# A cross-attention and ternary feed-forward kernel on one core: new hand-written orders for all engines, new PSUM banks, and a finer warm-up

## The chip, the cores and the metric

The kernel runs on one core of a Trainium2 chip. The metric is the device time of one execution in microseconds; the time of a kernel is the median of its runs. One execution of each kernel is also recorded by the hardware profiler, and the views below come from that execution. Engines are called by their names in the profile: PE is TensorE's matmuls, PEld its weight loads, DVE is VectorE, ACT is ScalarE, POOL is GpSimd, SP is SyncE, which only issues transfers.

## The reference, cut to what matters

Eight batches of 256 rows and 512 columns. A linear attention against a context, then a feed-forward block with ternary weights:

```
q, k, v = heads(norm(x) @ Wq + bq), heads(ctx @ Wk + bk), heads(ctx @ Wv + bv)   # 16 heads of 32
q', k'  = relu(q @ Wqf), relu(k @ Wkf) * mask                                    # 64 features a head
out     = (q' @ (k'^T v)) / (q' @ sum(k') + 1e-8)
x1      = x + out @ Wo + bo
xq      = quant8(norm(x1))                      # scale 127 / max|row|, round
z       = (xq @ tern(Wu)) * relu(xq @ tern(Wg))^2          # 2048 wide
y       = quant8(subln(z) * g)
result  = x1 + y @ tern(Wd)
tern(W) = clip(round(W / mean|W|), -1, 1) * mean|W|
```

## The kernel before

All is tiled to 128 partitions. The 2048 rows of `x` are 16 tiles `i` (two to a batch `a`); the 2048-wide middle of the feed-forward block is worked in halves of 1024 columns, so there are 32 units `u = 2 * i + h`. The attention runs in fp32 precision by splitting each operand into a high part and the rest, with three matmuls for each product (`products`, L356 to L360).

The program has one function per engine, `tensor`, `scalar`, `vector`, `gpsimd` and `sync`. Each defines small steps and then calls them in a fixed order written out by hand, with loops only over repeated steps. Each step waits for semaphores (named signals, such as `z_rows.at(u)`), does one or a few instructions and raises its own signal. Nothing reorders at run time: an engine works its list from top to bottom, and an instruction that waits holds back all behind it. On TensorE the list also carries extra waits in the calls, as in `up(15, 1, z_rows.at(30))`: they free the PSUM bank that the step is going to overwrite. Which bank each step writes is in tables at the top (`K_BANK`, `Q_BANK`, `G_BANK`, `U_BANK`, `D_BANK` and so on); gates and up projections take two neighbouring banks of the eight, from the number in the table on.

The stages, in order of time:

- **Start** (0 to 17 us). `warm` runs matmuls on zeros. The weights of the keys come in four slices, the context of batch 0 in four; ScalarE rounds each to its high part (`key_weights_hi`, L642, `context_hi`, L638), VectorE subtracts (`key_weights_lo`, `context_lo`), and `keys_first` multiplies them slice by slice. It begins with the high part of context slice 0 and weight slice 0.
- **Key stage** (to about 117 us). For each batch `b`: `keys`, `values`, `key_features`, `key_values`. ScalarE copies keys out of PSUM (`key_rows`) and the sums (`key_values_copy`, L678), VectorE values and features (`value_rows`, `key_feature_rows`). In between, ScalarE and VectorE turn the three feed-forward matrices ternary, each in four slices of 1 MB that share four slots with other weights: `magnitudes` (L668) sums absolute values while it copies, `total` adds them over partitions on TensorE, `scaled_weights`, `rounded_weights` and `ternary` finish. A slot is loaded again as soon as it was read.
- **Mixed stage** (to about 377 us). TensorE interleaves, for later batches, `transpose`, `queries`, `query_features`, `attend` and `project`, and for earlier tiles `gate`, `up` and `down`. One unit goes as follows: `gate` and `relu` (L718), `relu_squared` (L722), `gated` (L983, VectorE: up projection times squared gate, into `zb` or `zbe`), `sum_of_squares` (L726), `weighted` (times the sublayer weight, on VectorE L990 or on GpSimd L1198), `largest` (L994), then after both halves of a tile a chain of small columns on GpSimd, `y_scale` on VectorE, `scaled_y` and `rounded_y` (VectorE or ScalarE), a transposing transfer (`turn_y`), `down`, `result` and `store`. The tuples `Y_ON_DVE`, `YK_ON_DVE`, `YB_ON_DVE` and their partners say which engine multiplies, scales and rounds each unit.
- **End.** Gates and up projections of tiles 13 to 15, then `down(11)` to `down(14)` and `down_last`, whose two halves wait for two half transposes of tile 15 (`turn_y_half`).

The few lines that say how a gated product frees a bank, and who waits:

```python
dve.wait_ge(*rr_rows.at(u)); dve.wait_ge(*ups_done.at(u))
dve.tensor_tensor(z, two_banks(U_BANK[u]), r_place(u)[:, :], ALU.mult).then_inc(*z_rows.now(u))
```

## Time and profile before

| what | us |
| --- | --- |
| median of 3 runs | 425.06 (424.82 to 425.75) |
| the profiled execution | 424.21 |
| its span, first to last instruction | 422.4 |
| PE busy | 407.8 |
| PEld busy | 283.4 |
| DVE busy | 338.5 |
| ACT busy | 290.3 |
| POOL busy | 152.6 |

The profiled execution's time is its span and 1.8 us around it. Busy time counts instructions from start to end; matmuls overlap each other, so their pace is the distance of their starts. A wait in the timeline stands in brackets behind the instruction that came after it, with the engine and line that ended it. The granted clock of TensorE is full over the whole span.

### The profile page before, as it was taken

The page shows a single profiled execution, that of the slowest core. Times are in us where ns is not written, and L with a number is a line of the kernel's source. Part 1 is how long each engine was busy: PE and PEld are TensorE (multiplying, and loading weights), DVE is VectorE, ACT ScalarE, POOL GpSimd, SP SyncE. Part 2 cuts the span into 40 slices and gives each one's busy share as a digit, 9 for nine tenths or more (in the row PEclk, how much of TensorE's full clock was granted, in tenths as well). Part 3 has the DMA queues.
Part 4 walks back from the last instruction along what each step waited for, and adds up shares of the span by engine and source line. Part 5 has one row for each costly group of instructions (what it writes and reads, how often), then busy time and mean ns, then how long its engine had stood idle before and what let it go on. Part 6 is the DMA issues. An engine that isn't in the chain of part 4 may idle for free.

```text
span 422.4 us, 11313 instructions
## 1 busy us (share of the span) xinstructions
PE 407.8 (97%) x4822; PEld 283.4 (67%) x4851; DVE 338.5 (80%) x501; ACT 290.3 (69%) x409; POOL 152.6 (36%) x291
## 2 busy tenths in 40 slices
PE   7999999999999999999999999999998999999986
PEld 7889889988978757645944764584575576464333
DVE  4734949478369999999996998897999698997993
ACT  5676989891273396787479549578772958939970
POOL 0000000006025653652655255454359034447630
PEclk9999999999999999999999999999999999999999
DMA  7992747450050300330212033034021021411346
GB/s 258 421 383 91 292 161 265 189 199 5 3 225 13 104 16 0 64 87 26 51 52 50 30 59 89 25 64 90 15 62 37 14 51 36 95 46 25 62 99 164
DMA packets 51170, 42.42 MB, mean 100 GB/s; under 512 B 43056, under 2 KB 44080, under 8 KB 49200
## 3 DMA queue, kind: packets, MB, share of 16 engines
q1 hardware_dynamic: 50544, 41.18, 32.1%
q8 instruction: 38, 0.62, 0.6%
q10 hardware_dynamic: 576, 0.52, 0.4%
q14 instruction: 12, 0.10, 0.1%
HBM read 27.01 MB, written 4.19 MB: 74 GB/s over the span
## 4 chain that ended last, share of the span: by engine, by line
PE 41%; DVE 30%; issue 8%; ACT 8%; POOL 7%; DMA 4%; SPq 0%; DVEq 0%; POOLq 0%
PE ps L408 9%; PE ps L539 7%; PE ps L556 6%; DVE zb L983 5%; PE ps L358 4%; PE ps L360 4%; PE ps L359 4%; DVE tk L994 3%; DMA xs<-in_wg_dram 2%; DVE zb L990 2%; POOL zb L1198 2%; ACT rb L726 2%; PE ps L515 2%; PE ps L430 2%; PE ps L449 2%
## 5 line engine op out<-in xcount | busy, mean ns | idle before, releaser
L539 PE MATMUL ps<-tu,xqT 128*128 128x512 bf16 x248 | 59.0, 379 | 2.3 <-DVE zb L983 1.2
L539 PE MATMUL ps<-tg,xqT 128*128 128x512 bf16 x242 | 57.8, 379 | 2.0 <-issue 1.3
L556 PE MATMUL ps<-td,yqT 128*128 128x512 bf16 x202 | 46.1, 379 | 2.4 <-DVE zbe L983 1.2
L539 PEld LDWEIGHTS ps<-tu,xqT 128*128 128x128 bf16 x256 | 23.9, 98 | 32.6 <-issue 2.6
L539 PEld LDWEIGHTS ps<-tg,xqT 128*128 128x128 bf16 x256 | 23.8, 98 | 31.0 <-issue 4.5
L983 DVE TENSOR_TENSOR zb<-ps,rb 128x1024 f32<-128x1024 f32 x29 | 35.3, 1218 | 9.4 <-ACT rb L722 8.9
L726 ACT ACTIVATE rb<-zb 128x1024 f32<-128x1024 f32 x29 | 30.6, 1054 | 17.1 <-DVE zb L983 16.9
L994 DVE TENSOR_REDUCE tk<-zb 128x1 f32<-128x1024 f32 x30 | 36.2, 1209 | 3.1 <-POOL zb L1198 3.0
L1198 POOL TENSOR_TENSOR zb<-zb,g_b 128x1024 f32<-128x1024 f32 x11 | 27.2, 2470 | 29.2 <-ACT rb L726 26.4
L556 PEld LDWEIGHTS ps<-td,yqT 128*128 128x128 bf16 x208 | 19.7, 98 | 26.8 <-DVE zbe L983 1.7
L358 PE MATMUL ps<-aph,wqh 128*128 128x256 f32 x128 | 36.8, 287 | 0.0
L718 ACT ACTIVATE rb<-ps 128x1024 f32<-128x1024 f32 x29 | 29.6, 1021 | 9.4 <-PE ps L539 8.2
L359 PE MATMUL ps<-apl,wqh 128*128 128x256 f32 x128 | 35.9, 281 | 0.0
L360 PE MATMUL ps<-aph,wql 128*128 128x256 f32 x128 | 35.9, 281 | 0.0
L358 PE MATMUL ps<-aph,wkh 128*128 128x256 f32 x124 | 35.3, 285 | 0.0
L360 PE MATMUL ps<-aph,wkl 128*128 128x256 f32 x124 | 34.6, 279 | 0.0
L359 PE MATMUL ps<-apl,wkh 128*128 128x256 f32 x124 | 34.6, 279 | 0.0
L722 ACT ACTIVATE rb<-rb 128x1024 f32<-128x1024 f32 x29 | 30.7, 1059 | 0.5
L711 ACT ACTIVATE xq<-xq,cm,tk 128x512 f32<-128x512 f32 x16 | 13.0, 812 | 25.0 <-DVE tk L969 24.9
L990 DVE TENSOR_TENSOR zb<-zb,g_b 128x1024 f32<-128x1024 f32 x19 | 27.4, 1440 | 0.0
L358 PE MATMUL ps<-woh,qoh 128*128 128x512 f32 x64 | 26.9, 421 | 0.0
L408 PE MATMUL ps<-woh,aph 128*128 128x512 f32 x64 | 25.8, 403 | 0.0
(154 smaller groups left out, 1043.3 us busy)
## 6 DMA issues: line engine op xcount, KB each, us to landing
xs<-in_wg_dram SPq DMA_DIRECT2D x4, 1024.0 KB, 14.4
xs<-in_wu_dram SPq DMA_DIRECT2D x4, 1024.0 KB, 5.5
xs<-in_wd_dram SPq DMA_DIRECT2D x4, 1024.0 KB, 7.7
xs<-in_x_dram SPq DMA_DIRECT2D x8, 512.0 KB, 4.6
out_dram<-xs SPq DMA_DIRECT2D x15, 256.0 KB, 2.2
craw<-in_ctx_dram SPq DMA_DIRECT2D x7, 512.0 KB, 5.6
xs<-in_wk_dram SPq DMA_DIRECT2D x4, 256.0 KB, 4.8
xs<-in_wv_dram SPq DMA_DIRECT2D x4, 256.0 KB, 6.5
```

The costliest lines, as they stand in the source:

```text
L358: pe.matmul(out, lh, rh, start=first, stop=False)
L359: pe.matmul(out, lh, rl, start=False, stop=False)
L360: return pe.matmul(out, ll, rh, start=False, stop=end)
L408: k = pe.matmul(ps[:, 4 + t, :], left[:, cs], right[:, kc, :], start=n == 0, stop=n == 11)
L539: k = pe.matmul(ps[:, b0 + n, :], xqT[:, i % 3, kc, :], tern[w][:, o:o + 512], start=kc == 0, stop=kc == KC - 1)
L556: k = pe.matmul(ps[:, D_BANK[i], :], yqT(i)[:, j, :], tern[2][:, 512 * j:512 * j + 512], start=j == 0, stop=j == 15)
L722: act.activation(r_place(u)[:, :], r_place(u)[:, :], ACT.Square).then_inc(*rr_rows.now(u))
L726: act.activation(r_place(u)[:, :], z_place(u)[0], ACT.Square, accum_out=col(S0 + u % 2, u // 2)).then_inc(*z_squares.now(u))
L983: dve.tensor_tensor(z, two_banks(U_BANK[u]), r_place(u)[:, :], ALU.mult).then_inc(*z_rows.now(u))
L990: dve.tensor_tensor(z, z, g_b[:, HF * (u % 2):HF * (u % 2) + HF], ALU.mult).then_inc(*y_dve.now(u))
L994: dve.tensor_reduce(col(M0 + u % 2, u // 2), z_place(u)[0], AX_X, ALU.max, apply_absolute_value=True).then_inc(*y_largest.now(u))
L1198: pool.tensor_tensor(z, z, g_b[:, HF * (u % 2):HF * (u % 2) + HF], ALU.mult).then_inc(*y_pool.now(u))
```

## The change

All five lists are written in another order, all PSUM banks are assigned anew, and with that the bank waits in TensorE's calls. Besides this:

- The warm-up runs 41 matmuls of 113 columns in place of 29 of 160.
- The keys of a batch, always in banks 6 and 7 before, get their banks from a table, and the copies follow.
- One unit's multiply moves from GpSimd to VectorE on balance (21 and 11 for 20 and 12); VectorE scales 19 units for 17 and rounds 17 for 19, ScalarE the others.
- The slices of the gate and up matrices are loaded and worked in another order (3, 1, 0, 2), and the sum of their magnitudes waits for whichever slice is last.
- The value weights are issued ahead of the small constants, and the context of batch 1 behind the features and the value bias.

```diff
-WARM = 29
+WARM = 41
...
-                    k = pe.matmul(ps[:, 7, 0:160], zeros[:, 0:128], zeros[:, 128:288], start=True, stop=True)
+                    k = pe.matmul(ps[:, 7, 0:113], zeros[:, 0:128], zeros[:, 128:241], start=True, stop=True)
...
+K_BANK = ((), (6, 7), (5, 4), (4, 5), (4, 5), (7, 6), (5, 7), (4, 6))
-KV_BANK = (0, 0, 0, 0, 0, 0, 0, 6)
+KV_BANK = (1, 6, 0, 0, 0, 2, 5, 0)
...
-                    out = ps[:, 6 + oq // 2, T * (oq % 2):T * (oq % 2) + T]
+                    out = ps[:, K_BANK[b][oq // 2], T * (oq % 2):T * (oq % 2) + T]
...
-            keys(1); values(1, 0, range(12), v_rows.at(0, 0)); key_values(0); values(1, 1, range(12))
-            key_features(1, (0, kvc_rows.at(0, 0)), (1, kvc_rows.at(0, 1))); keys(2); total(0); key_values(1)
+            values(1, 0, range(3), ctx_lo.at(1, 0)); keys(1); key_values(0); values(1, 0, range(3, 12))
+            values(1, 1, range(12)); key_features(1, (1, kvc_rows.at(0, 0)), (2, kvc_rows.at(0, 1)))
+            keys(2, v_rows.at(1, 1)); total(0, kT_rows.at(2, 1)); key_values(1); values(2, 0, range(12), kT_rows.at(2, 3))
...
-            up(15, 1, z_rows.at(30)); down(11); down(12, z_rows.at(31)); down(13); down(14); down_last(out_rows.at(12, 0))
+            gate(15, 0, z_rows.at(28)); up(15, 0, r_rows.at(29)); gate(15, 1); up(15, 1, z_rows.at(30)); down(11)
+            down(12, r_rows.at(31)); down(13, z_rows.at(31)); down(14); down_last(out_rows.at(12, 0))
...
-            sum_of_squares(19); scaled_x(11); query_rows(6, 2); query_rows(6, 3); relu(20)
+            query_rows(6, 1); scaled_x(10); query_rows(6, 2); query_rows(6, 3); scaled_x(11); relu(20)
...
-                dve.wait_ge(*w_abs.at(w, 3))
+                dve.wait_ge(*w_abs.at(w, W_LAST[w]))
```

ScalarE at the start of the program, before and now. `wkh<-xs` is a slice of the key weights, `aph<-craw` a slice of the context (128x256 for batch 0, 128x1024 for the others), `kT<-ps` the key rows.

```order
L642 ACTIVATE wkh<-xs 128x512
L638 ACTIVATE aph<-craw 128x256
L642 ACTIVATE wkh<-xs 128x512
L638 ACTIVATE aph<-craw 128x256
L642 ACTIVATE wkh<-xs 128x512
```

```order
L646 ACTIVATE wkh<-xs 128x512 x2
L642 ACTIVATE aph<-craw 128x256 x2
L646 ACTIVATE wkh<-xs 128x512
L642 ACTIVATE aph<-craw 128x256 x2
L646 ACTIVATE wkh<-xs 128x512
```

The first context slice, for which TensorE waits, now comes behind two weight slices and no longer behind one.

ScalarE in the key stage, where the keys of batch 1 and the first key-value sums are copied, before and now. `tg,wsum<-xs` is a magnitude pass over a slice of the gate matrix, `kvc<-ps` the copy of the sums.

```order
L664 ACTIVATE kT<-ps,small 128x256 x3
L668 ACTIVATE tg,wsum<-xs 128x2048
L678 ACTIVATE kvc<-ps 128x132 x2
L668 ACTIVATE tg,wsum<-xs 128x2048
L638 ACTIVATE aph<-craw 128x1024
```

```order
L668 ACTIVATE kT<-ps,small 128x256 x4
L682 ACTIVATE kvc<-ps 128x132
L672 ACTIVATE tg,wsum<-xs 128x2048
L682 ACTIVATE kvc<-ps 128x132
L672 ACTIVATE tg,wsum<-xs 128x2048
L642 ACTIVATE aph<-craw 128x1024
```

One of the two copies moved ahead of the magnitude pass.

VectorE at the end, from the product gated(29) on, before and now. `zb<-ps,rb` and `zb<-ps,rbe` are gated products, `zb<-zb,g_b` the multiply by the sublayer weight (of unit 28 here), `tk<-zb` a maximum, `yqb<-zb` a rounding.

```order
L983 TENSOR_TENSOR zb<-ps,rbe 128x1024
L998 RECIPROCAL sy<-tk 128x1
L1002 TENSOR_TENSOR tk<-sy,tk 128x1
L1007 TENSOR_SCALAR zb<-zb,tk,cm 128x1024
L1013 TENSOR_SCALAR yqb<-zb 128x1024
L983 TENSOR_TENSOR zb<-ps,rb 128x1024
L990 TENSOR_TENSOR zb<-zb,g_b 128x1024
```

```order
L989 TENSOR_TENSOR zb<-ps,rbe 128x1024
L1004 RECIPROCAL sy<-tk 128x1
L1008 TENSOR_TENSOR tk<-sy,tk 128x1
L1013 TENSOR_SCALAR zb<-zb,tk,cm 128x1024
L1019 TENSOR_SCALAR yqb<-zb 128x1024
L996 TENSOR_TENSOR zb<-zb,g_b 128x1024
L989 TENSOR_TENSOR zb<-ps,rb 128x1024
```

The multiply of unit 28 now stands ahead of gated(30), for which TensorE's last up projection waits, and no longer behind it.

## Rows read from the trace of the kernel before

**Rows 1.** The page, part 1: busy us, share of the span, instructions

```profile
PE 407.8 (97%) x4822; PEld 283.4 (67%) x4851; DVE 338.5 (80%) x501; ACT 290.3 (69%) x409; POOL 152.6 (36%) x291
```

**Rows 2.** Timeline of PE near the end: start us, us, engine line op

```profile
392.98 1.89 PE L539 MATMUL ps<-tu,xqT 128*128 128x512 bf16 x8
394.70 1.89 PE L539 MATMUL ps<-tg,xqT 128*128 128x512 bf16 x8
```

**Rows 3.** Busy time by stretch: us, PE, PEld, DVE, ACT, POOL, clock, DMA

```profile
140.00:220.00 80.00, 77.97 (x607) 48.97 (x614) 76.71 (x121) 56.67 (x83) 42.91 (x92) 1.00 0.19 44
```

**Rows 4.** Timeline of the start, of ACT and of PE

```profile
4.79 0.63 ACT L642 ACTIVATE wkh<-xs 128x512 fp32r<-128x512 f32 x1 [0.68 <-DMA xs<-in_wk_dram]
5.32 0.40 ACT L638 ACTIVATE aph<-craw 128x256 fp32r<-128x256 f32 x1
5.70 0.63 ACT L642 ACTIVATE wkh<-xs 128x512 fp32r<-128x512 f32 x1
...
12.79 1.06 ACT L638 ACTIVATE aph<-craw 128x1024 fp32r<-128x1024 f32 x1
...
1.24 3.52 PE L353 MATMUL ps<-xn 128*128 128x160 bf16 x29 [1.24 <-DVE xn L833]
5.78 0.72 PE L367 MATMUL ps<-aph,wkh 128*128 128x256 f32 x4 [1.01 <-ACT aph L638]
```

**Rows 5.** Timeline of the key stage, of ACT and of PE

```profile
29.62 1.92 ACT L668 ACTIVATE tg<-xs 128x2048 bf16<-128x2048 f32 x1
...
31.94 1.71 PE L430 MATMUL ps<-fkr,kT 32*64 32x64 f32 x128 [0.52 <-ACT kvc L678]
39.15 0.28 PE L457 MATMUL ps<-vt,wst 128*128 128x1 f32 x2
39.52 1.32 PE L449 MATMUL ps<-vt,kp 128*32 128x33 f32 x128
```

**Rows 6.** A gate slice's transfer in the chain, and the page's part 6 (median)

```profile
22.71 10.12 DMA xs<-in_wg_dram
...
xs<-in_wu_dram SPq DMA_DIRECT2D x4, 1024.0 KB, 5.5
```

**Rows 7.** Timeline of PE at three waits of the mixed stage

```profile
181.74 3.63 PE L556 MATMUL ps<-td,yqT 128*128 128x512 bf16 x16 [0.61 <-DVE zb L983]
...
327.21 1.09 PE L494 MATMUL ps<-qT,fkr 32*64 32x256 f32 x24 [0.68 <-ACT qT L689]
...
379.15 1.90 PE L539 MATMUL ps<-tu,xqT 128*128 128x512 bf16 x8 [0.29 <-DVE xs L945]
```

**Rows 8.** VectorE's multiplies and roundings: duration ns min/median/max

```profile
L990 DVE TENSOR_TENSOR zb<-zb,g_b x19: 1192/1216/3170, 159.4 to 404.3; 128x1024 f32<-128x1024 f32 x19
L1013 DVE TENSOR_SCALAR yqb<-zb x18: 661/693/1803, 173.5 to 411.0; 128x1024 bf16<-128x1024 f32 x18
```

**Rows 9.** Timeline of the end, by engine

```profile
404.18 3.63 PE L556 MATMUL ps<-td,yqT 128*128 128x512 bf16 x16 [1.25 <-DVE zbe L983]
417.67 1.92 PE L569 MATMUL ps<-td,yqTq 128*128 128x256 bf16 x16 [0.73 <-DMA yqTq<-yqb]
...
397.44 3.17 DVE L990 TENSOR_TENSOR zb<-zb,g_b 128x1024 f32<-128x1024 f32 x1
402.90 1.22 DVE L983 TENSOR_TENSOR zbe<-ps,rbe 128x1024 f32<-128x1024 f32 x1
406.57 1.21 DVE L994 TENSOR_REDUCE tk<-zb 128x1 f32<-128x1024 f32 x1
...
396.99 1.23 ACT L731 ACTIVATE zbe<-zbe,cm,tk 128x1024 f32<-128x1024 f32 x1
398.25 1.15 ACT L737 ACTIVATE yqb<-zbe,cm 128x1024 bf16<-128x1024 f32 x1
399.31 1.00 ACT L718 ACTIVATE rbe<-ps 128x1024 f32<-128x1024 f32 x1
...
397.17 2.36 POOL L1198 TENSOR_TENSOR zb<-zb,g_b 128x1024 f32<-128x1024 f32 x1 [2.83 <-ACT rbe L726]
...
414.15 1.29 SPq L1312 DMA_TRANSPOSE yqTq<-yqb  x1
```

More of the change, by code:

```diff
@@ L585, in tensor @@
-            key_features(6, (0, kvc_rows.at(5, 0)), (1, kvc_rows.at(5, 1))); transpose(0)
-            values(7, 0, range(4), v_rows.at(6, 0)); transpose(1, v_rows.at(6, 1)); values(7, 0, range(4, 12))
-            key_values(6); queries(0, 0); queries(0, 1); values(7, 1, range(6)); query_features(0, (3, v_rows.at(7, 0)))
-            values(7, 1, range(6, 12)); attend(0, (0, qf_rows.at(0, 1))); keys(7)
-            key_features(7, (0, attended.at(0, 0)), (3, attended.at(0, 1))); transpose(2); project(0); transpose(3)
@@ new lines, in tensor @@
+            key_features(5, (0, kvc_rows.at(4, 0)), (1, kvc_rows.at(4, 1))); keys(6, v_rows.at(5, 1))
+            key_values(5, kf_rows.at(5, 3)); values(6, 0, range(12)); values(6, 1, range(12), kT_rows.at(6, 1))
+            key_features(6, (2, kvc_rows.at(5, 0)), (3, kvc_rows.at(5, 1))); transpose(0); transpose(1, v_rows.at(6, 1))
+            values(7, 0, range(12), ctx_lo.at(7, 0)); queries(0, 0); queries(0, 1, v_rows.at(7, 0)); key_values(6)
+            query_features(0, (2, qT_rows.at(0, 3))); values(7, 1, range(12), kvc_rows.at(6, 0)); attend(0)
@@ new lines, in tensor @@
+            up(4, 0); gate(4, 1, r_rows.at(8)); up(4, 1, qf_rows.at(3, 2)); attend(3, (1, z_rows.at(8)))
+            gate(5, 0, r_rows.at(9)); up(5, 0, z_rows.at(9)); gate(5, 1, r_rows.at(10)); down(3, den_error.at(3, 0))
+            transpose(8, r_rows.at(11)); transpose(9); project(6); up(5, 1, xT_lo.at(9)); queries(4, 1)
+            queries(4, 0, z_rows.at(11)); project(7); down(4); query_features(4, (0, qT_rows.at(4, 1)), (2, x1_rows.at(7)))
+            gate(6, 0); up(6, 0, qf_rows.at(4, 2)); attend(4, (1, qf_rows.at(4, 3)), (2, r_rows.at(12)))
@@ new lines, in tensor @@
+            gate(6, 1, out_rows.at(4, 0)); up(6, 1, z_rows.at(12)); down(5, den_error.at(4, 0))
+            gate(7, 0, attended.at(4, 1)); project(8); up(7, 0); transpose(10); gate(7, 1, x1_rows.at(8))
+            transpose(11, r_rows.at(14)); project(9); up(7, 1, xT_lo.at(10)); queries(5, 0); queries(5, 1, z_rows.at(15))
+            down(6); query_features(5); gate(8, 0, out_rows.at(6, 0)); up(8, 0, qf_rows.at(5, 2)); attend(5)
+            gate(8, 1, r_rows.at(16)); up(8, 1, z_rows.at(16)); down(7, r_rows.at(17)); gate(9, 0, attended.at(5, 1))
@@ new lines, in tensor @@
+            up(9, 0); transpose(12); project(10); transpose(13); gate(9, 1, r_rows.at(18)); up(9, 1, out_rows.at(7, 0))
+            queries(6, 0, xT_lo.at(13)); project(11); down(8, x1_rows.at(10)); queries(6, 1, z_rows.at(19))
+            gate(10, 0, out_rows.at(8, 0)); query_features(6, (2, qT_rows.at(6, 3))); up(10, 0)
+            attend(6, (1, qf_rows.at(6, 2))); gate(10, 1); up(10, 1, z_rows.at(20)); transpose(14, den_error.at(6, 1))
+            transpose(15, attended.at(6, 0)); gate(11, 0, r_rows.at(21)); project(12); queries(7, 0, xT_lo.at(15))
@@ L806, in scalar @@
+            sum_of_squares(14); transposed_hi(11); relu(15); relu_squared(15); scaled_x(8); sum_of_squares(15)
+            for n in range(4):
+                query_rows(5, n)
+            scaled_y(15)
             for n in range(4):
                 query_feature_rows(5, n)
-            relu(16); scaled_x(9); relu_squared(16); inverse_root(5, 0); inverse_root(5, 1); inverse_guess(5, 0)
-            inverse_guess(5, 1); sum_of_squares(16); relu(17); relu_squared(17); attended_hi(5, 0); attended_hi(5, 1)
@@ L1110, in gpsimd @@
+            largest(28); largest(29); gated(31); y_scale(14); factor(14); weighted(30); weighted(31); rounded_y(28)
+            largest(30); largest(31); result(11); y_scale(15); factor(15); scaled_y(30); rounded_y(30); scaled_y(31)
+            for n in range(12, 15):
+                result(n)
+            result(15, 0); result(15, 1)
         def gpsimd(pool):
@@ L1200, in gpsimd @@
             set_ones(); set_constants(); weight_product()
-            for n in range(5):
+            for n in range(4):
                 x_rstd(n)
@@ L1263, in load_query_weights, with load_sublayer_weight, load_ffn_weights @@
                 sp.dma_start(slot[2], wq_d).then_inc(*slot_in[2].now("Wq"))
-            def load_sublayer_weight():
+            def load_sublayer_weight(*late):
+                for after in late:
+                    sp.wait_ge(*after)
                 sp.dma_start(g_b[:, :], g_d).then_inc(*g_in.now())
-            def load_ffn_weights(w, c):
+            def load_ffn_weights(w, c, *late):
                 s = slot_of[c]
+                for after in late:
+                    sp.wait_ge(*after)
                 if w:
```

438 lines of the change are left out of this document (208 added, 230 removed).

## The prediction

> **What bounds the kernel now.** I read the page's busy times first, then TensorE's pace in the timeline, then the stretch around each of its waits, and last the end. TensorE is busy 407.8 us, 97% of the span of 422.4 [rows 1]. A busy figure alone proves little, since matmul ends are modelled; the pace is better. Blocks of eight 128x512 matmuls start at 392.98 and 394.70, so 1.72 us apart or some 216 ns each, with nothing between them [rows 2]. TensorE's queue is thus the clock of this program, and a new order wins only where that queue stands still: 14.6 us in all, start and end included. VectorE is nearly full from 140 to 220 us, 76.7 of 80 [rows 3]; there a late VectorE operation reaches TensorE soon.
>
> The computation keeps its matmuls. What counts is the sum of standstills, place by place.
>
> **1. The start: a loss.** ScalarE now rounds the second slice of the key weights ahead of the first context slice. Before, it took a weight slice at 4.79, the context at 5.32, the next weight slice at 5.70 with no wait for its load, and TensorE's first real matmul started at 5.78, on the context [rows 4]. One weight slice of 0.53 us (5.32 - 4.79, start to start) now stands ahead of the context, so the first matmul comes at 6.31: **+0.53 us**. It can't be less, as the load lands when it did; VectorE's swap of the same pair is the same shift, not a second one.
>
> The warm-up has 41 matmuls of 113 columns in place of 29 of 160, 4633 columns for 4640. If columns set the pace it ends as before. If each matmul's weight load sets it, 41 times the mean pace of the row (3.52 us by 29, 0.12) end near 6.2, still before 6.31 [rows 4]. Nothing at both ends, covered by the wait for the first slices; without that cover 1.4 us. The context of batch 1 is now issued behind features and biases. Before, ScalarE read it at 12.79 without waiting [rows 4]; now it reads it behind all four key-row operations of batch 0, later than before by more than two issues take. Nothing.
>
> **2. The key stage: two waits go.** TensorE stood 0.52 us before 31.94, because the copy of the first key-value sums sat on ScalarE behind a magnitude pass of 1.92 us from 29.62 [rows 5]. Now one copy stands ahead of a magnitude pass and the other behind one only, some 2 us before TensorE asks: **-0.52 us**. The matmul of 39.15 was followed by key-values at 39.52 only, for VectorE's key features were late [rows 5]. VectorE's magnitude sum, on which they queued, now asks for a load that lands when it did, and by the durations the features are then done 1.5 us before TensorE wants them: **-0.32 us**. The new arrangement has a price: keys now also use banks 4 and 5, those of the values, so the values of batch 3 wait for key rows that stand on ScalarE behind two magnitude passes. Adding up passes of 1.92 us from [rows 5], those rows come 0.5 us before TensorE asks. If an up-weight slice took as long as the last gate slice (10.12 us) in place of the median of 5.5 [rows 6], this would cost 4.6 - 0.5 = 4.1 us. I take nothing, since the up slices are nearest to their own median, and keep 4.1 as the far end.
>
> **3. The middle: three waits undone by name.** At 181.74 down(0) had waited 0.61 us for gated(4), in whose bank it wrote; its new bank is freed by an older feature copy. At 327.21 query features had waited 0.68 us for two query rows that stood on ScalarE behind scaled_x(11); the scaling now stands behind the rows. At 379.15 an up projection had waited 0.29 us for a residual; the gate after it takes that wait now [rows 7]. That is 1.58 us if nothing else appears. But the whole list is new and most bank waits have new partners, so I take half, **-0.8 us**, with -1.6 as the near end and +0.8 (as much new as was there) as the far one. VectorE's load helps: of units 0 to 15 it now rounds 8 and no longer 10, 0.69 us each [rows 8], just where it is full; ScalarE, with 23 of 80 us free there [rows 3], takes them.
>
> **4. The end.** TensorE stood before the last up projection, for gated(30), and 1.25 us before down(12), for gated(31) [rows 9]. The second wait falls away: down(12) has another bank, and down(13), 3.5 us later, asks for gated(31). This alone buys nothing, since TensorE waits for the last transpose again at 417.67. The end is set by the chain gated(31), multiply, two maxima, factor, scale, round, transpose, 16 matmuls. What delays it is VectorE's multiply at 397.44, which took 3.17 us [rows 9] where the median is 1.22 [rows 8]. GpSimd ran its own multiply from 397.17, 2.36 us long [rows 9]; it ended at 399.5, and VectorE's ended 1.1 us after that.
>
> The new order puts this multiply ahead of gated(30), takes one rounding (1.15 us) off ScalarE ahead of it, and sums the squares of unit 29 before it squares unit 30. Walked with the durations of [rows 8, 9] from the gates of unit 14 on: gated(29) ends at 393.3, scale and round at 395.1, the multiply runs 395.1 to 396.3, gated(30) to 397.5, so TensorE's wait before the last up projection stays. Two maxima end at 400.0; gated(31) needs ScalarE's relu and square, which end at 400.4, and runs to 401.6 in place of 404.1. Two multiplies, one added rounding (it waits for ScalarE's scaling until 404.0) and two maxima end at 407.1; factor, scale, round and the second scaling, now VectorE's, at 410.7; ScalarE rounds to 411.9, and the last transpose goes out at 412.0 and not 414.15. With the 3.5 us from its issue to the matmuls at 417.67 [rows 9], TensorE starts its last 16 at 415.4; its own queue, without the wait at down(12), is done with the rest by then. **-2.3 us**.
>
> **Sum.** +0.53 - 0.52 - 0.32 - 0.8 - 2.3 = -3.4 us. The profiled execution took 424.21 us (the span and 1.8 around it), 0.85 below the median of 425.06; on the median the forecast is **421.6 us**.
>
> **Rivals.** *A, GpSimd gets there first.* GpSimd's multiply of unit 29 becomes ready when ScalarE has summed its squares, by the same walk at 395.1, as VectorE's does. Whoever is second is held for the other's whole length, as at 397.44. If that is VectorE, gated(30) ends near 399.9 and TensorE loses 2.4 us before its last up projection. The last transposes still gain some 1.2 us, but TensorE, with the last up projection, four down blocks and the last one still to do, ends only 0.2 earlier: +0.53 - 0.84 - 0.8 - 0.2 = -1.3, **423.8 us**. For it: the two times are equal within my error. Against: VectorE gets there with nothing else to do. The Trainium skill has a rule on this in SBUF — State Buffer, section "SBUF: two separate sides": the port pair that the two share is an exclusive lock, kept for the whole instruction by whichever starts first while the other fully blocks. By that rule the time is 421.6 or 423.8 and nothing between; if both merely slowed each other it would be some 422.7. The trace agrees with the rule at 397.44, with 3.17 us.
>
> *B, the holds fall elsewhere (slower).* VectorE's multiplies reach 3.17 us against a median of 1.22, its roundings 1.80 against 0.69 [rows 8]. The new list moves every one of them. In the full stretch VectorE has 3.3 us to spare [rows 3], so a multiply held there in front of a gated product (3.17 - 1.22 = 1.95 us) passes to TensorE nearly whole. Two of them, and the race of A lost, give 423.8 + 3.9 = **427.7 us**. From 2.2 us of new standstill on (1.3 + 0.85) it decides. For: VectorE takes one multiply and two scalings more of units 16 to 31. Against: it has room in that half.
>
> *C, the waits move and don't go.* Every list is fixed, so a wait removed on one engine can come back on another. If the middle costs 2.3 us more than I take, the end's gain is used up and the time is **423.9 to 425 us**. For: at 97% busy there is little to win, and step 2 narrowed slacks to half a microsecond. Against: the end's gain comes last, and nothing behind it can lose it.
>
> **Chances.** Forecast 0.45, A 0.20, B 0.18, C 0.17. A measurement of this kernel can tell about 0.2% (0.85 us) from no change, so faster is below 424.2: the forecast, most of A (0.15) and a little of C (0.03), 0.63. Same takes 0.05 of A and 0.13 of C, 0.18. Slower is B with a remnant of C, 0.19. The forecast's own range is 419.9 to 423.4 (the middle's two ends, less than a microsecond for the rest). With A, C and the near part of B, where one hold and not two strikes, the range is **419.9 to 426.2 us**.
>
> **What would show it.** Right: the first real matmul near 6.3; no wait near 32 and 39; VectorE's multiply before gated(30) at 1.2 us; one wait before the last up projection and none before down(12); the last 16 matmuls 3 to 4 us earlier. A is right if that multiply takes over 2 us and the last up projection waits 3 us. B shows as long multiplies between 140 and 220 with TensorE idle behind gated products, C as bank waits of TensorE for features, rows or results. I am wrong in step 3 if TensorE's idle time between 140 and 390 has grown, and in step 1 if the first matmul hasn't moved.

## The result, and the profile after

The change made the kernel **slower**: 429.24 us at the median (427.39 to 430.30, 5 runs) beside 425.06 (424.82 to 426.05, 5 runs), a ratio of 1.0097 with a 95% interval of 1.0077 to 1.0117. I had forecast 421.6 and a range that ended at 426.2. The profiled execution took 429.24 us, its span 427.2, 4.8 more than before.

The page's part 1 for the changed kernel, to be held against [rows 1]:

```profile
PE 409.0 (96%) x4834; PEld 285.5 (67%) x4863; DVE 336.7 (79%) x502; ACT 289.9 (68%) x409; POOL 151.3 (35%) x290
```

The busy times say almost nothing: TensorE's matmuls have 1.2 us more, its weight loads 2.1, the other engines less. The time lies in what TensorE waits for. The view of waits of the changed kernel (engine, output, line, what ended the wait: us in total, times, longest):

```profile
PE ps L460 <- DVE wst L883: 2.5, 1, 2.5
PE ps L544 <- DVE xs L1025: 2.2, 2, 1.7
PE ps L370 <- ACT aph L642: 1.6, 1, 1.6
...
PE ps L361 <- DVE xn L930: 1.6, 1, 1.6
...
PE ps L544 <- DVE zb L989: 1.1, 1, 1.1
PE ps L497 <- DVE xs L1025: 0.9, 1, 0.9
```

In the order of time they are: the first real matmul (L370), the total of the up weights (L460), the keys of batch 7 (L361), the query features of batch 3 (L497), the first gates of tiles 8 and 10 (L544 for L1025, a result), and the last up projection (L544 for L989). In the timeline of TensorE (start us, us, line, operation, idle before and what ended it) four of them:

```profile
6.47 0.74 PE L370 MATMUL ps<-aph,wkh 128*128 128x256 f32 x4 [1.61 <-ACT aph L642]
...
64.96 0.38 PE L460 MATMUL ps<-vt,wst 128*128 128x1 f32 x2 [2.49 <-DVE wst L883]
...
128.77 0.36 PE L361 MATMUL ps<-aph,wkh 128*128 128x256 f32 x1 [1.58 <-DVE xn L930]
...
297.16 1.89 PE L544 MATMUL ps<-tg,xqT 128*128 128x512 bf16 x7 [1.70 <-DVE xs L1025]
```

Two of them cost more than they show. Busy time of TensorE by stretches of the changed kernel (us, TensorE's busy time, granted clock, DMA share, GB/s):

```profile
6.00:7.00 1.00, 0.53 (x4) 1.00 0.85 281
7.00:8.00 1.00, 0.98 (x7) 0.81 1.06 392
8.00:9.00 1.00, 1.00 (x6) 0.50 0.96 297
9.00:10.00 1.00, 1.00 (x7) 0.50 1.00 351
10.00:11.00 1.00, 1.00 (x7) 0.50 1.07 390
11.00:12.00 1.00, 1.00 (x10) 0.98 1.08 419
...
65.00:66.00 1.00, 1.00 (x58) 0.82 0.00 0
66.00:67.00 1.00, 1.00 (x88) 0.50 0.06 16
67.00:68.00 1.00, 1.00 (x30) 0.50 0.00 0
68.00:69.00 1.00, 1.00 (x7) 0.50 0.62 188
69.00:70.00 1.00, 1.00 (x10) 0.97 0.84 336
```

Shortly after the first matmul, and again after the wait for the total, the clock stands at 0.50, the lower of its two levels (1.2 GHz for 2.4), for some 3.3 us. With the full clock a row of one microsecond counts 10 to 12 of the 128x256 matmuls, here 6 or 7; from start to start they lie 0.21 us apart and not 0.11. The kernel before had 1.00 in every such microsecond. **TensorE counts as 100% busy all the while**, so that no busy figure shows this.

With both traces laid side by side, by the start of the same group of matmuls, the difference grows so (before, after):

| place | before | after | difference |
|---|---|---|---|
| values of batch 0 | 11.67 | 13.95 | +2.28 |
| key-values of batch 2 | 53.82 | 55.48 | +1.66 |
| total of the up weights | 60.65 | 64.96 | +4.31 |
| key-values of batch 3 | 68.23 | 73.79 | +5.56 |
| attention of batch 1 | 148.96 | 154.80 | +5.84 |
| query features of batch 7 | 358.00 | 365.83 | +7.83 |
| down(11) | 399.32 | 406.76 | +7.44 |
| end of the span | 422.4 | 427.2 | +4.8 |

So 5.6 us were lost by 74 us, 0.3 more by the attention of batch 1, 2.0 more in the middle, and 3.0 came back after the last query features. The end did what was forecast, to be held against [rows 9]:

```profile
402.61 1.22 DVE L996 TENSOR_TENSOR zb<-zb,g_b 128x1024 f32<-128x1024 f32 x1
...
402.62 3.43 POOL L1204 TENSOR_TENSOR zb<-zb,g_b 128x1024 f32<-128x1024 f32 x1 [1.28 <-ACT rbe L730]
...
405.02 1.90 PE L544 MATMUL ps<-tu,xqT 128*128 128x512 bf16 x8 [1.12 <-DVE zb L989]
...
420.58 3.85 PE L574 MATMUL ps<-td,yqTq 128*128 128x256 bf16 x32
```

VectorE began its multiply 0.01 us ahead of GpSimd and took 1.22 us in place of 3.17; GpSimd paid instead, with 3.43. TensorE stands before the last up projection only, and the last 32 matmuls run without a wait.

### The profile page after: what moved, and what is told of

Read it like the earlier page. It is cut to its first block, busy times and chain, and to the rows that moved or that the text cites. A ratio compares the mean times of both kernels' runs of the same rounds, so it can differ in the third digit from the quotient of the medians.

```text
span 427.2 us, 11340 instructions
## 1 busy us (share of the span) xinstructions
PE 409.0 (96%) x4834; PEld 285.5 (67%) x4863; DVE 336.7 (79%) x502; ACT 289.9 (68%) x409; POOL 151.3 (35%) x290
## 4 chain that ended last, share of the span: by engine, by line
PE 64%; DVE 15%; ACT 8%; issue 6%; DMA 4%; POOL 2%; SPq 0%; DVEq 0%; ACTq 0%
PE ps L544 15%; PE ps L361 8%; PE ps L363 8%; PE ps L362 8%; PE ps L411 7%; PE ps L561 7%; PE ps L518 3%; PE ps L433 3%; DVE zb L989 3%; DMA xs<-in_wu_dram 2%; PE ps L452 2%; PE ps L497 1%; ACT rb L722 1%; DVE zb L996 1%; ACT rb L730 1%
## 5 line engine op out<-in xcount | busy, mean ns | idle before, releaser
L544 PE MATMUL ps<-tg,xqT 128*128 128x512 bf16 x240 | 57.5, 379 | 4.8 <-DVE xs L1025 2.2
L544 PE MATMUL ps<-tu,xqT 128*128 128x512 bf16 x250 | 59.2, 379 | 1.7 <-DVE zb L989 1.1
L544 PEld LDWEIGHTS ps<-tg,xqT 128*128 128x128 bf16 x256 | 23.5, 98 | 34.8 <-issue 8.0
L544 PEld LDWEIGHTS ps<-tu,xqT 128*128 128x128 bf16 x256 | 24.1, 98 | 31.6 <-issue 2.2
L989 DVE TENSOR_TENSOR zb<-ps,rb 128x1024 f32<-128x1024 f32 x29 | 35.3, 1219 | 9.6 <-ACT rb L726 8.4
L1204 POOL TENSOR_TENSOR zb<-zb,g_b 128x1024 f32<-128x1024 f32 x10 | 26.0, 2604 | 36.3 <-ACT rb L730 35.0
L361 PE MATMUL ps<-aph,wkh 128*128 128x256 f32 x124 | 36.0, 291 | 1.6 <-DVE xn L930 1.6
L361 PE MATMUL ps<-aph,wqh 128*128 128x256 f32 x128 | 36.9, 288 | 0.0
L872 DVE TENSOR_TENSOR vt<-ps,bo_b 128x512 f32<-128x512 f32 x16 | 11.0, 687 | 30.2 <-PE ps L411 30.2
L1140 POOL TENSOR_TENSOR xs<-xs,bo_b 128x512 f32<-128x512 f32 x16 | 21.4, 1350 | 25.5 <-DMA bo_b<-in_bo_dram 19.8
L361 PE MATMUL ps<-woh,qoh 128*128 128x512 f32 x64 | 26.6, 416 | 0.0
```

What stands on the lines that cost most here:

```text
L361: pe.matmul(out, lh, rh, start=first, stop=False)
L544: k = pe.matmul(ps[:, b0 + n, :], xqT[:, i % 3, kc, :], tern[w][:, o:o + 512], start=kc == 0, stop=kc == KC - 1)
L1204: pool.tensor_tensor(z, z, g_b[:, HF * (u % 2):HF * (u % 2) + HF], ALU.mult).then_inc(*y_pool.now(u))
```

## The experiments

The theory after the result: the new end is worth some 3 us, and the loss is made of a few single waits (start, total, keys of batch 7, first gate of tile 8), of which the first two also let the clock fall. The rival: the new order as a whole is worse, with VectorE late everywhere, so that a wait removed comes back. Ratios are against runs of the kernel before on the same chip in the same job; its medians there were 424.46 (e1 to e4), 424.96 (e5 to e8) and 424.87 (e9 to e12). A ratio goes by all runs and can differ from the quotient of the two medians by 0.1%. The diffs below are cut to the calls that change.

| run | edit | us | ratio, 95% |
|---|---|---|---|
| e1 | change, old start order | 427.45 | 1.0078 (1.0054 to 1.0101) |
| e2 | change, 60 warm-ups | 429.76 | 1.0113 (1.0091 to 1.0135) |
| e3 | change, up slice early | 426.73 | 1.0044 (1.0022 to 1.0065) |
| e4 | change, keys(7) in other banks | 428.53 | 1.0090 (1.0060 to 1.0120) |
| e5 | change, four repairs | 421.53 | 0.9928 (0.9907 to 0.9948) |
| e6 | before, new order at its end | 423.55 | 0.9965 (0.9952 to 0.9977) |
| e7 | before, 20 warm-ups | 427.06 | 1.0054 (1.0039 to 1.0069) |
| e8 | change, down(6) in another bank | 429.51 | 1.0115 (1.0096 to 1.0135) |
| e9 | e5 and down(2) in another bank | 421.63 | 0.9919 (0.9900 to 0.9938) |
| e10 | before, up slice late | 430.16 | 1.0114 (1.0093 to 1.0134) |
| e11 | e5 with the new start | 423.92 | 0.9965 (0.9950 to 0.9980) |
| e12 | e5 with the old end | 423.34 | 0.9963 (0.9949 to 0.9976) |

### The start: e1, e2, e7, e11

e1, the old start in the changed kernel (ScalarE's list here; VectorE's got the same order back):

```
-table(); key_weights_hi(0); key_weights_hi(1); context_hi(0, 0); context_hi(0, 1); key_weights_hi(2)
-context_hi(0, 2); context_hi(0, 3); key_weights_hi(3)
+table(); key_weights_hi(0); context_hi(0, 0); key_weights_hi(1); context_hi(0, 1); key_weights_hi(2)
+context_hi(0, 2); key_weights_hi(3); context_hi(0, 3)
...
```

> The changed kernel, with only the first batch's rounding order on ScalarE and VectorE put back (weight slice, context slice, weight slice, ...), the 41 warm-up matmuls kept. In the changed kernel the first real matmul stood at 6.47 (5.78 before), the granted clock fell to 0.50 from 8 to 11 us, and values of batch 0 began 2.28 us later than before (13.95 for 11.67). Theory 1 (the clock fell because the idle stretch between warm-up and first matmul grew from 1.01 to 1.61 us; shift 0.7 and clock 1.6): first matmul near 5.8, clock 1.00 throughout, values at 11.7 to 11.9, and about 2.3 us less at the end: 427.0. Theory 2 (the narrower warm-up matmuls, 113 columns for 160, did not raise the clock for good): the clock still falls; only the 0.7 goes: 428.5. Rival to both: the 2.3 us are absorbed by the wait for the last up slice before the total of the up weights, which then grows by what the start gains: 429.2 with a longer wait at 62 us.

The idle stretch was 0.97 us and the first microseconds had a clock of 1.00; values of batch 0 began at 12.14, 1.8 earlier. But at the end of the profiled span only 0.7 was left, because the falls had moved. (The ratios of e1 and of the change, 1.0078 and 1.0097, have intervals that overlap, so that the times alone don't show a gain.) The wait for the total was still 1.6 us and the clock fell behind it; then it fell behind the keys of batch 7 too, where the changed kernel had waited nearly as long (1.58) without a fall:

```profile
126.56 0.35 PE L361 MATMUL ps<-aph,wkh 128*128 128x256 f32 x1 [1.81 <-DVE xn L930]
```

```profile
63.00:64.00 1.00, 1.00 (x81) 0.50 0.09 16
64.00:65.00 1.00, 1.00 (x40) 0.50 0.00 0
128.00:129.00 1.00, 1.00 (x6) 0.50 0.00 0
129.00:130.00 1.00, 1.00 (x7) 0.50 0.00 0
```

The spread between runs goes with the falls. A run's mean granted clock counts them, since 3.3 us at half in 427 take 0.004 off: e1's twelve runs lie at 425.29 and 427.21 with a clock of 1.00, at 426.68 to 427.59 with 0.996 and at 428.31 to 431.12 with 0.992. The kernel before read 1.00 or 0.999 in each of its 56 runs in these three jobs. A wait behind which the clock may fall makes a kernel slower and its time uncertain. The traces were taken of one run each; what the falls of the other runs followed isn't recorded.

e2, a longer warm-up:

```
-WARM = 41
+WARM = 60
```

> The changed kernel with 60 warm-up matmuls of 113 columns in place of 41, which at some 73 ns each (13 to 14 of them in each us) end near 6.25 and not 4.85, just ahead of the first real matmul. Theory 1 (idle stretch): the clock stays at 1.00, the first matmul stays at 6.47, the values of batch 0 begin near 12.35 (13.95 less 1.6), and the time is 1.6 us less: 427.6. Theory 2 (narrow matmuls): the clock falls as it did: 429.2. Rival: the gain of the start is taken up by the wait for the last up slice at 62 us, whose load does not hang on TensorE: 429.2 at a clock of 1.00.

The warm-up now ran up to the first real matmul, which came at 6.63 with no idle time ahead of it, and there was no fall in the start; values of batch 0 began at 12.49, 1.46 earlier. So it is not the width of the warm-up matmuls. The time didn't move: there was a fall behind the wait for the total (1.6 us long) and one behind the keys of batch 7 (2.2 us).

e7, a shorter one in the kernel before:

```
-WARM = 29
+WARM = 20
```

> The kernel before with 20 warm-up matmuls of 160 columns in place of 29, so that the warm-up ends near 3.9 and TensorE idles some 1.9 us (1.01 before) ahead of its first real matmul; nothing else is moved. Theory (an idle stretch of about 1.6 us or more, and not the width of the matmuls or the order, lets the granted clock fall to 0.50 for 3.3 us soon after): the clock falls between 6 and 12 us, the values of batch 0 begin 1.6 us later than 11.67, and the time is 1.6 us more than before: 426.1 at a granted clock of 0.996. Rival (the fall comes from the new order or the narrow matmuls): the clock stays at 1.00 and the time is that of before: 424.5.

The time came out as expected (+0.54%), the record only in part. Values of batch 0 began at 13.59, 1.9 us later than before, but the granted clock reads 1.00 there:

```profile
5.69 1.22 PE L367 MATMUL ps<-aph,wkh 128*128 128x256 f32 x4 [1.61 <-ACT aph L638]
...
8.42 0.41 PE L358 MATMUL ps<-aph,wkh 128*128 128x256 f32 x1
8.63 0.41 PE L359 MATMUL ps<-apl,wkh 128*128 128x256 f32 x1
...
10.76 0.28 PE L358 MATMUL ps<-aph,wkh 128*128 128x256 f32 x1
10.87 0.28 PE L359 MATMUL ps<-apl,wkh 128*128 128x256 f32 x1
```

0.21 us from start to start at first, which is 256 columns at 1.2 GHz, and 0.12 later. The engine hadn't yet left the lower level, and the column of the clock shows 1.00 until its first change. So e7 shows what slow matmuls at the start cost; it doesn't show a clock that falls behind an idle stretch, since here it hadn't risen. The Trainium skill, TensorE: Matmul & The Clock Gate, section "What's actually happening", says that the throttled state is where the engine starts and that activity releases it; the pace in this trace agrees. e8 (below), whose start is that of the change, had this too: its warm-up and its real matmuls ran at the lower level up to 10.3, behind a wait of only 1.18 us, and values of batch 0 began at 13.85. The new start thus lost its time in one of two ways, by a fall or by a clock that hadn't risen.

e11, the kernel of the four repairs (e5, below) without the edit of e1, so with the new start:

> The kernel of the four repairs (e5) with the first batch's rounding order as in the change (two weight slices ahead of the first context slice). In e5 values of batch 0 began at 11.92. Theory (the new start costs its shift of 0.5 us and, the idle stretch before the first real matmul being 1.5 us or more, matmuls at 213 ns in place of 113 for some 3.3 us): they begin at 13.9, and the time is 2.0 us more than that of e5: 423.5. Rival 1 (only the shift of the prediction, +0.5): 422.0. Rival 2 (waits later in the key stage absorb it): 421.5.

Values of batch 0 began at 13.91 (11.92 in e5), the wait was 1.75 us and the clock 0.50 from 8 to 10. By the medians it is 2.4 us slower than e5, by the ratios 1.6, and in the traces 2.0 at this place: **the new start costs some 2 us, where I had put 0.53.** Of its twelve runs the two with a clock of 1.00 took 422.68 and 423.25, the ten with 0.996 or less 423.26 to 424.17.

### The last up slice: e3 and e10

e3 in the changed kernel:

```
-load_ffn_weights(1, 1); load_ffn_weights(1, 0); load_context(6); load_ffn_weights(1, 2); load_context(7)
+load_ffn_weights(1, 1); load_ffn_weights(1, 0); load_ffn_weights(1, 2); load_context(6); load_context(7)
...
-ternary(0, 1); value_rows(2, 1); rounded_weights(0, 0)
+ternary(0, 1); value_rows(2, 1); rounded_weights(0, 0); rounded_weights(0, 2)
...
-context_lo(4, 0); rounded_weights(0, 2); ternary(0, 2); ternary(0, 0)
+context_lo(4, 0); ternary(0, 2); ternary(0, 0)
```

> The changed kernel, with the last up-weight slice loaded ahead of the context of batch 6 in SyncE's list, and the rounding that frees its place moved on VectorE from behind the key features of batch 2 and a context slice to ahead of them (from 53.58 to about 50.1). In the changed kernel the load was issued at 54.83 and landed near 62.7, and TensorE stood 2.49 us before the total of the up weights (64.96), for VectorE's sum. Theory: it is issued near 51.4, lands at 59 or before, the sum is done near 61.3 and the wait of 2.49 us is gone; nothing after it takes it back, for the key stage runs without another wait of that size: 426.8. Rival 1: the load is slow because the queue is full (it took 7.9 us, the median of its row is 5.7), and issued earlier it lands hardly earlier: 428.5. Rival 2: key features of batch 2 come 1.2 us later and the key-values of batch 2 now wait: up to 0.5 us back, 427.3.

The wait is gone, with the fall behind it. In the changed kernel the slice was asked for at 54.83 and ScalarE stood 3.54 us for it:

```profile
53.58 1.22 DVE L895 TENSOR_SCALAR tg<-xs 128x2048 bf16<-128x2048 f32 x1
...
53.69 0.33 SPq L1252 DMA_DIRECT2D craw<-in_ctx_dram  x1
54.83 0.33 SPq L1289 DMA_DIRECT2D xs<-in_wu_dram  x1
```

```profile
62.71 1.91 ACT L672 ACTIVATE tu<-xs 128x2048 bf16<-128x2048 f32 x1 [3.54 <-DMA xs<-in_wu_dram]
```

The first of these lines is the rounding that frees the slice's place. It ended at 54.80, and the load was issued 0.03 us later; the context ahead of it in the queue had been issued at 53.69 already. **What released the late load was thus the rounding, and not its turn in the queue.** e3 and e10 move both at once, so that no run shows either alone. By these rows the queue without the late rounding would have held the load to some 54.0 (53.69 and the 0.33 of that issue, an estimate), so that the repair needs both moves.

In e3 the rounding is done near 51.0, all four slices are issued before the context, the last near 51.1, and ScalarE takes it with no wait:

```profile
45.01 6.38 SPq L1289 DMA_DIRECT2D xs<-in_wu_dram  x4
54.59 0.33 SPq L1252 DMA_DIRECT2D craw<-in_ctx_dram  x1
```

```profile
59.05 1.91 ACT L672 ACTIVATE tu<-xs 128x2048 bf16<-128x2048 f32 x1
```

The total ran at 61.83 (3.1 earlier) and the key-values of batch 3 at 69.21 (4.6 earlier, of which 0.5 was there before the wait): wait and clock together. The median is 2.5 us under the change's, less than the 3.8 between the two spans, since one fall more or less moves a run by 1.6.

e10 puts the same two moves into the kernel before, which had the slice rounded near 48.7 and asked for at 50.0:

```
-rounded_weights(0, 2); rounded_weights(0, 3)
+rounded_weights(0, 2)
...
-context_lo(4, 0); ternary(0, 2)
+context_lo(4, 0); rounded_weights(0, 3); ternary(0, 2)
...
-for n in range(4):
-    load_ffn_weights(1, n)
-load_context(6); load_context(7)
+for n in range(3):
+    load_ffn_weights(1, n)
+load_context(6); load_ffn_weights(1, 3); load_context(7)
```

> The kernel before with only the term under dispute put in: the rounding that frees the place of the last up slice stands behind the key features of batch 2 and a context slice (about 53.5 and not 48.7), and its load is issued behind the context of batch 6. Theory: the load is issued near 54.6, lands at 61 to 62.5, VectorE's sum is done near 63.5 and TensorE stands 2.5 to 3 us before the total of the up weights, which began at 60.65; behind that wait the granted clock falls to 0.50 for 3.3 us or more, which costs another 1.6, since no wait of over 1.3 us was in this kernel and no fall either. Time: 424.7 + 2.7 + 1.6 = 429.0 at a clock of 0.996 or less; without the fall 427.4 at 1.00. Rival (in the order before there is slack behind it, since the waits at 129, 144 and 181 us are for other engines that gain by it): 425.5.

```profile
64.62 0.38 PE L457 MATMUL ps<-vt,wst 128*128 128x1 f32 x2 [2.81 <-DVE wst L877]
```

Here too the load was issued, at 54.55, 0.03 us behind the end of the rounding (53.30 and 1.22 long). The kernel is 5.3 us slower by the medians, 4.8 by the ratio, with the clock at 0.50 from 67 to 69. By the key-values of batch 3 TensorE was 5.95 us behind the kernel before, 1.0 of which it had lost by 47.5, ahead of anything that the edit moves; from there on it stayed between 5.9 and 6.2 to the end. So **nothing later takes a loss of the key stage back**, which had been my rival here. The Trainium skill, TensorE: Matmul & The Clock Gate, section "HAM oscillation — how this bites in real kernels", describes a kernel in which a wait for a load puts TensorE back to the lower level and the ramp is paid again; e10 agrees in kind, with some 1.5 us of slow matmuls, though its wait of 2.8 us is shorter than those given there.

### Bank waits: e4, e8, e9

e4, the keys of batch 7 in another bank:

```
-K_BANK = ((), (6, 7), (5, 4), (4, 5), (4, 5), (7, 6), (5, 7), (4, 6))
+K_BANK = ((), (6, 7), (5, 4), (4, 5), (4, 5), (7, 6), (5, 7), (4, 5))
...
-keys(7, den_error.at(0, 0))
+keys(7, v_rows.at(7, 1))
```

> The changed kernel with the keys of batch 7 in banks 4 and 5 in place of 4 and 6, behind the value rows of batch 7 in place of the first denominator's error. In the changed kernel TensorE stood 1.95 us there (127.14 to 129.10, 1.6 of it put down to VectorE's L930). Theory: the wait is gone or below 0.3 us, since those value rows stand two operations ahead of that error in VectorE's list, and the time is 1.6 us less: 427.6. Rival: VectorE and ScalarE are the ones that are late there (the attention of batch 0 must be divided out before the key features of batch 7 and the projection can start), so the 1.6 us come back before the key features, the projection or the first gate: 429.2, with a new wait between 133 and 150 us.

The rival was right. The wait of L361 is gone and the keys come 2.3 us earlier (1.6 gained here), but by the attention of batch 1 (153.96 for 154.80) only 0.8 of it all was left. It came back as several short waits, the longest 0.54 us, before the key-values:

```profile
139.38 1.33 PE L452 MATMUL ps<-vt,kp 128*32 128x33 f32 x128 [0.54 <-DVE kp L879]
```

e8: down(6) in bank 7 in place of 3, and the wait for its result moved from `gate(8, 0)` to `attend(5)`:

```
-down(6); query_features(5); gate(8, 0, out_rows.at(6, 0)); up(8, 0, qf_rows.at(5, 2)); attend(5)
+down(6, x1_rows.at(9)); query_features(5); gate(8, 0); up(8, 0, qf_rows.at(5, 2)); attend(5, (0, out_rows.at(6, 0)))
```

> The changed kernel with only the product of down(6) moved from bank 3 to bank 7, which is free there, and the wait for its result moved from the first gate of tile 8 to the attention of batch 5. Theory (the 2.07 us before that gate are a bank wait that buys nothing): the wait is gone, the attention waits below 0.3, and the time is 1.5 to 2 us less at the same granted clock: 427.4. Rival (VectorE is late there, the 40 us before are its fullest, and TensorE 2 us earlier meets the next of its products): the waits for results, gated products or query features between 297 and 335 grow by what is gained: 429.2.

The median says that nothing was gained. The trace says otherwise: e8 was 2.1 us behind the changed kernel at the query features of batch 5, mostly because its clock had stayed at 0.50 for more than six microseconds around and behind the total, and only 0.35 behind at the next up projection (299.23 for 298.88). The four microseconds around the first gate of tile 8 (297.50 here) are filled:

```profile
296.00:300.00 4.00, 4.00 (x47) 1.00 0.00 1
```

**The wait, 1.7 us in the change, was a bank's alone and is worth its length in this trace**; a longer fall hides it there. Nothing was given back behind it: e8 was still 0.34 behind at the last query features.

e9, on top of e5 (and `D_BANK[2]` is 0 in place of 5):

```
-query_features(3, (0, out_rows.at(2, 0)))
-up(4, 0)
+query_features(3)
+up(4, 0, out_rows.at(2, 0))
```

> The kernel of the four repairs (e5) with one more: the product of down(2) in bank 0 and no longer in bank 5, so that the query features of batch 3 don't wait for its result (0.9 us there in the repaired kernel) and the first up projection of tile 4, 2.2 us later, asks for it. Theory (a bank wait that buys nothing, as at down(6)): the 0.9 us go, and nothing takes them back: 420.7, granted clock 1.00. Rival (VectorE, at its fullest there, is behind in all that follows): the wait turns up at the up projection or at the next gated product, 421.5.

The wait of 0.9 us is gone and half of it came back: against its own state at 190 us the kernel was 1.0 us ahead of e5 at the query features of batch 3 and 0.5 ahead from the attention of batch 4 on. The times (421.63 and 421.53) can't tell the two apart.

### The end: e6 and e12

e6, three edits in the kernel before:

```
-scaled_y(26); rounded_y(26); gated(30); weighted(28)
+scaled_y(26); rounded_y(26); weighted(28); gated(30)
...
-relu(30); relu_squared(30); sum_of_squares(29)
+relu(30); sum_of_squares(29); relu_squared(30)
...
-down(12, z_rows.at(31)); down(13)
+down(12, r_rows.at(30)); down(13, r_rows.at(31))
```

with `D_BANK[12] = 1` in place of 7.

> The kernel before with only three edits at its end: VectorE's multiply of unit 28 ahead of gated(30) and not behind it, ScalarE's sum of squares of unit 29 ahead of the square of unit 30, and the product of down(12) in bank 1, which is free, so that it no longer waits for gated(31). Theory (term 4 of the prediction: the end is set by the chain from gated(31) to the last transpose, delayed by the multiply of 3.17 us): the multiply takes 1.2, gated(31) comes some 2 us earlier than 402.90, and the end 2.0 to 2.3 us: 422.3. Rival 1: GpSimd's multiply of unit 29 gets its operands first and the held multiply is before gated(30): no gain or a small loss, 424.0 to 424.8. Rival 2: without the wait at down(12) the last 16 matmuls simply wait longer for the transposes: below 0.5 us, if the chain is not what sets them.

Mechanism right, size smaller: 1.4 us by the median. VectorE's multiply took 1.22 us and GpSimd's, which the record has 0.01 us ahead of it, 3.45; gated(31) began at 402.50 in a profile that had been 1.1 us behind the kernel before since 147, so some 1.5 earlier by its own state; but the wait before the last up projection grew from 0.98 to 1.90 us. e12 is the reverse, the first two of these edits undone in e5:

> The kernel of the four repairs (e5) with two edits of its end undone: VectorE's multiply of unit 28 behind gated(30) again, and ScalarE's sum of squares of unit 29 behind the square of unit 30 again; banks as in e5. Theory (the order of these operations is worth most of the gain at the end): gated(30) comes 1.1 us earlier and the wait before the last up projection (1.13 us) goes, but the multiply is held by GpSimd's of unit 29 and takes 2.4 to 3.2 us in place of 1.22, gated(31) begins 0.7 to 2.0 us later than 399.61, and the time is 0.7 to 2.0 us more than that of e5: 422.9. Rival (the bank of down(12) is what was gained, the order of VectorE is not): 421.5, with no wait of TensorE above 0.5 us between 390 and 410.

```profile
397.77 3.18 DVE L996 TENSOR_TENSOR zb<-zb,g_b 128x1024 f32<-128x1024 f32 x1
```

```profile
397.51 2.36 POOL L1204 TENSOR_TENSOR zb<-zb,g_b 128x1024 f32<-128x1024 f32 x1 [2.37 <-ACT rbe L730]
```

```profile
415.98 3.85 PE L574 MATMUL ps<-td,yqTq 128*128 128x256 bf16 x32 [1.51 <-DMA yqTq<-yqb]
```

The held multiply is back, with 3.18 us, and TensorE stands 1.51 us for the last transposes. 1.8 us slower than e5 by the medians, 1.5 by the ratios. The Trainium skill's rule on the port shared by VectorE and GpSimd (SBUF — State Buffer, "SBUF: two separate sides"), on which rival A rested, agrees where two such multiplies meet at the end: one takes its own 1.22 or 2.36 us and the other is held, to 3.17 in the kernel before, 3.18 in e12 (VectorE, 0.27 and 0.26 us behind), 3.43 in the change and 3.45 in e6 (GpSimd). That the first one wins shows where the starts are 0.26 us apart; where they are 0.01 apart the records can't tell who was first.

### All repairs together: e5

The edits of e1, e3, e4 and e8 in one kernel.

> The changed kernel with four local repairs and nothing else: the old rounding order of the first batch, the last up slice loaded ahead of the context of batch 6 with its rounding moved ahead, the keys of batch 7 in banks 4 and 5, and the product of down(6) in bank 7 and no longer in bank 3, so that the first gate of tile 8 (which stood 2.07 us, 295.41 to 297.49) doesn't wait for its result; the attention of batch 5 now asks for that bank. Theory (the new tail is worth 2.3 us or more, and the loss of the changed kernel came from four places, each a wait and, where it was above 1.5 us, a stretch of 3.3 us at a granted clock of 0.50): no wait above 1.5 us is left but the load of the first weights, the granted clock of the run is 1.00, and the time is 429.2 - 1.8 (start) - 3.8 (up slice with its clock) - 0.7 (keys) - 1.5 (down(6)) = 421.4, so 0.993 of before. Rival 1 (the order as a whole is worse in its middle, beyond these places): 424 to 425, with new waits of TensorE between 150 and 400 in the place of those removed. Rival 2: TensorE comes 7 us earlier to the middle and loads and VectorE are late there: 423.

**421.53 us, 0.7% below the kernel before and, by the two ratios, 1.7% below the change**, with a clock of 1.00 in all six runs (420.99 to 423.99). Besides the 1.2 us ahead of the warm-up no wait of TensorE is above 1.13 us:

```profile
PE ps L544 <- DVE zb L989: 1.1, 1, 1.1
PE ps L497 <- DVE xs L1025: 0.9, 1, 0.9
PE ps L544 <- DMA xqT<-xqb: 0.9, 2, 0.6
PE ps L544 <- DVE xs L1025: 0.6, 1, 0.6
```

Against the kernel before it is 0.6 us ahead at the attention of batch 1, 0.4 at the last query features and 3.4 at the end of the span. This is close to the forecast for the change itself, reached once four places are mended. Singly, e1, e3, e4 and e8 differ from the change's ratio by -0.19, -0.53, -0.07 and +0.18%, -0.6% in sum; together they give -1.7%. They don't add up: where one wait was mended alone, the clock fell behind another (e1, e2). Its own start isn't yet good: the warm-up ran at the lower level to its end, and the first real matmuls too, 0.21 us from start to start for the first seven.

## Why the prediction was wrong

**Term 1, the start (+0.53; it was +2.28).** This step failed. The shift was 0.69 (5.78 to 6.47), close to the forecast. But I wrote of the warm-up "Nothing at both ends, covered by the wait", and looked only at when it ends, not at what the longer idle stretch behind it does: it went from 1.01 to 1.61 us, and 48 matmuls then took 7.48 us in place of 5.89. That is 1.6 us of slow matmuls at the lower level of the clock; the runs with the old start or with a warm-up up to the first real matmul don't have it (6.07 in e1, 5.86 in e2, 6.27 in e5), those with the new start do (7.46 in e11). No rival of mine had it.

**Term 2, the key stage (-0.84; it was +3.3 by the key-values of batch 3).** The wait at 31.94 went as forecast; between the values of batch 0 and the key-values of batch 2 0.6 us was gained of the 0.84. Then the step failed that let the up slices be: I costed a late slice by the length of its transfer (far end +4.1) and chose the median, and didn't follow its issue. The rounding that frees its place had moved on VectorE behind the key features and a context slice, to 53.58, and SyncE's list has the load behind the context of batch 6; it was issued as the rounding ended. That was 4.8 us later than before, and it was 7.9 us under way (the page's median is 5.7; the last slice of the kernel before took 7.9 too, from 49.99 to 57.88), so it came after TensorE had asked: 2.65 us, and 1.25 for the clock. e3 and e10 show it from both sides, with rounding and queue moved together.

**Between 74 and 149 us** I had forecast nothing. The keys of batch 7 wait 1.6 us for a denominator's error, but other parts of the stretch gain, and the sum is +0.3. By e4 most of this wait lies over VectorE's lateness and isn't a loss in itself.

**Term 3, the middle (-0.8, far end +0.8; it was +2.0).** The waits at 181.74 and 327.21 went (-0.8 and -1.3 around them). New ones are before the query features of batch 3 (0.93) and the first gate of tile 8 (1.70). That is rival C, waits that move, a little larger than I gave it (2.8 us more than my term for 2.3). The waits of TensorE between 140 and 390 that the views name add up to 4.3 us for 2.4 before, the sign that I had given of being wrong in this step. By e8 the bank of down(6) alone is 1.8 of it, and in e5, without it, the middle is 0.2 us longer than before.

**Term 4, the end (-2.3; it was -3.0).** Right in each link that I had named: multiply at 1.22, one wait before the last up projection, none before down(12), and no wait of the last matmuls. e12 puts 1.6 us of it on the order of VectorE and ScalarE there: from the last query features to the last 32 matmuls it took 56.35 us, e5 54.75.

**Rivals.** A didn't happen: VectorE's multiply took 1.22 us in all ten profiles with the new order (the change, e1 to e6, e8, e9, e11). But the two multiplies start within 0.02 us of each other in each of them, and my walk could not tell who would be first. That VectorE wins is repeatable here; why is not shown, and my choice of it was in part luck. B is refuted: VectorE's multiplies at L996 reach 1.50 us at most (3.17 in [rows 8]), its roundings 1.62 (1.80). That the kernel could become slower was on my list, but not for these reasons, a late load and the clock.

What was missing were two effects: when the place of a load comes free (which the order of VectorE's list shows), and the slow matmuls behind a long wait (of which the kernel before, with its clock at full, had no row).

## What to carry to other kernels

When an order changes, follow every load from the operation that frees its place through the list of the queue to its first reader; a load whose place came free 4.8 us later cost some 5 us here. Treat a wait of TensorE that grows beyond the waits the kernel had as costing more than its length, because slow matmuls may follow, and the run's mean granted clock tells how often they did. And compare two traces place by place before believing a median: e8's repair removed its wait for good while the time didn't change, and what e4's repair gained was given back soon after.

## What the runs showed of the hardware

- Falls of the clock to 0.50 stood behind waits of TensorE of 1.5 to 2.9 us (the start of the changed kernel and of e3, e4 and e11; the total in the changed kernel, e1, e2, e4, e8 and e10; the keys of batch 7 in e1 and e2), and cost 1.2 to 1.6 us each where I measured it (1.6 at the start and 1.25 behind the total in the changed kernel, 1.5 in e10), more in e8. They didn't stand behind all such waits: the keys of batch 7 in the changed kernel (1.58), e3 (1.9) and e8 (2.0), the first gate of tile 8 in the change (1.70) and the last up projection in e6 (1.90) had none. Which of them the clock follows isn't settled by these runs.
- The column of the granted clock reads 1.00 before its first change, even where matmuls run at the lower level (e7, e8, and the first seven real ones of e5), and a run's mean clock doesn't count such a start: e7's four runs read 1.00. The distance from one start to the next is the safer sign: 0.21 us for 256 columns at the lower level, 0.12 at the upper.
- A fall makes the time spread: in one job the kernel before stayed within 423.37 and 426.24 over 22 runs, and e1 lay between 425.29 and 431.12 over twelve.
